# A wait for TensorE's own third-last matmul, and two more semaphore instructions, ahead of each run of 256-column matmuls

## What is computed

```python
def attn(x, w_in, conv_w, conv_b, w_B, w_C, w_out):
    xp, z = split(x @ w_in, 2)                    # 256 -> 2 x 512
    xc = silu(causal_conv(xp, conv_w) + conv_b)   # 4 taps per channel
    h_t = 0.9 * h_{t-1} + 0.1 * (xc_t @ w_B)      # 16 states
    return ((h @ w_C) * silu(z)) @ w_out          # 512 -> 256

def ffn(x, Wr, br, W1, b1, W2, b2):
    idx = top_k(x[:, 0, :] @ Wr + br, 2)          # by the first token of a batch entry
    h = gelu(x @ W1[idx] + b1[idx])               # two experts, 256 -> 256 each
    return sum(h @ W2[idx] + b2[idx]) / 2

x = x + attn(layernorm(x), ...)
x = x + ffn(layernorm(x), ...)
```

## Time and profile before

| what | us |
|---|---|
| median of 3 runs | 509.01 (508.89 to 509.17) |
| the profiled execution, its own time | 509.31 |
| its span, first to last instruction | 507.5 |
| TensorE busy | 503.0 (99%) |
| VectorE busy | 452.3 (89%) |
| ScalarE busy | 400.7 (79%) |
| GpSimd busy | 348.2 (69%) |

### The profile page before, as it was taken

One profiled execution on the slowest core, in us unless ns is written; L12 is line 12 of the kernel. 1 busy time (PEld: TensorE's weight loads), 2 busy tenths in 40 slices (PEclk: granted clock), 3 DMA queues, 4 the chain that ended last, 5 costly groups with the idle time before them and its releaser, 6 DMA issues.

```text
span 507.5 us, 9839 instructions
## 1 busy us (share of the span) xinstructions
PE 503.0 (99%) x3026; PEld 447.6 (88%) x3026; DVE 452.3 (89%) x896; ACT 400.7 (79%) x692; POOL 348.2 (69%) x390
## 2 busy tenths in 40 slices
PE   8999999999999999999999999999999999999997
PEld 8889799898898989989899998989989899998997
DVE  6999899999998899989999899998999989996773
ACT  4986958878869788697887969779797887969454
POOL 4959597659693796928969197772977649673391
PEclk9999999999999999999999999999999999999999
DMA  8940005344251432606235170432604333130102
GB/s 266 292 174 12 32 0 173 119 131 162 74 182 37 165 124 83 206 17 193 79 124 165 42 223 24 165 124 86 203 40 143 106 125 125 51 115 0 43 3 83
DMA packets 53379, 57.28 MB, mean 113 GB/s; under 512 B 8682, under 2 KB 49642, under 8 KB 53226
## 3 DMA queue, kind: packets, MB, share of 16 engines
q1 hardware_dynamic: 51498, 56.67, 34.1%
q10 hardware_dynamic: 1856, 0.31, 0.3%
HBM read 35.46 MB, written 21.50 MB: 112 GB/s over the span
## 4 chain that ended last, share of the span: by engine, by line
PE 97%; DVE 1%; DMA 1%; issue 0%; DVEq 0%
PE blk L1291 16%; PE blk L1292 16%; PE blk L1296 16%; PE tok L1410 12%; PE tok L1408 12%; PE tok L1409 12%; PE turn L1449 3%; PE turn L1452 3%; PE blk L1471 3%; PE turn L1239 1%; PE tok L1291 1%; PE tok L1296 1%; PE tok L1292 1%; DMA x_mid<-in_L_attn_x 1%; DVE stats_t L914 0%; DVE normed L931 0%
## 5 line engine op out<-in xcount | busy, mean ns | idle before, releaser
L989 DVE SCALAR_TENSOR_TENSOR conv<-blk,tap_w,conv 128x512 f32<-128x512 f32 x192 | 130.1, 740 | 8.2 <-ACT conv L680 7.6
L485 POOL TENSOR_TENSOR y_lo<-gate,y_hi 128x512 fp32r<-128x512 f32 x57 | 72.2, 1299 | 36.6 <-ACT y_hi L608 36.5
L1291 PE MATMUL blk<-xn_hi,w_in_hi 128*128 128x512 f32 x228 | 89.5, 393 | 0.0
L1292 PE MATMUL blk<-xn_hi,w_in_lo 128*128 128x512 f32 x228 | 89.1, 391 | 0.0
L450 POOL TENSOR_TENSOR xc_lo<-conv,xc_hi 128x512 fp32r<-128x512 f32 x60 | 72.7, 1229 | 8.3 <-ACT xc_hi L608 8.1
L1408 PE MATMUL tok<-w_out_hi,y_hi 128*128 128x256 f32 x256 | 72.1, 282 | 0.0
L1410 PE MATMUL tok<-w_out_hi,y_lo 128*128 128x256 f32 x256 | 71.9, 281 | 0.0
L1409 PE MATMUL tok<-w_out_lo,y_hi 128*128 128x256 f32 x256 | 71.9, 281 | 0.0
L1296 PE MATMUL blk<-xn_lo,w_in_hi 128*128 128x512 f32 x228 | 70.3, 389 | 0.0
L1408 PE MATMUL tok<-w_hi,hid_hi 128*128 128x256 f32 x248 | 69.9, 282 | 0.0
L1410 PE MATMUL tok<-w_hi,hid_lo 128*128 128x256 f32 x248 | 69.7, 281 | 0.0
(11 more groups left out here) (189 smaller groups left out, 1321.7 us busy)
## 6 DMA issues: line engine op xcount, KB each, us to landing
spill<-normed SPq DMA_DIRECT2D x25, 512.0 KB, 2.8
normed<-spill SPq DMA_DIRECT2D x100, 128.0 KB, 2.8
out<-x_mid SPq DMA_DIRECT2D x30, 256.0 KB, 2.7
x_mid<-in_L_attn_x SPq DMA_DIRECT2D x29, 256.0 KB, 2.7
x_in<-in_L_attn_x SPq DMA_DIRECT2D x14, 512.0 KB, 4.3
w_all<-in_L_ffn_W SPq DMA_DIRECT2D x2, 2048.0 KB, 11.8
b_all<-in_L_ffn_b SPq DMA_DIRECT2D x1, 1024.0 KB, 13.1
gate<-in_L_attn_w_in SPq DMA_DIRECT2D x2, 256.0 KB, 4.5
```

Source lines behind the costliest of these rows:

```text
L485: nc.gpsimd.tensor_tensor(y_lo[:, j, :], gate_of(o, j), y_hi[:, j, :].bitcast(F32), ALU.subtract).then_inc(y_lo_set, 1)
L989: nc.vector.scalar_tensor_tensor(cols, blk[j][:], tap_w[:, j, t:t + 1], cols, ALU.mult, ALU.add).then_inc(tap_added, 1)
L1291: mm(dst, whi(k), his(k), start=(k == 0), stop=False)
L1292: mm(dst, wlo(k), his(k), start=False, stop=False)
```

## The change

TensorE gets three semaphores that only its own matmuls raise: `x_tail` after the fourth of the six matmuls of the last `xp` block, `state_tail` after the second of the four L1452 matmuls of `state_in`, and `up_tail` after the fourth matmul of the last `up` block in steps 16 and 17. Each time two 512-column matmuls are still to come behind the raised one, so it is the third-last of its run. A new function `behind()` stands after the old waits and ahead of the first 256-column matmul. It raises a counter `paced` that nobody waits for, waits for the tail semaphore, and raises `paced` three times more. In the built program that is four semaphore instructions: the first carries the old waits (done, y_lo_set or g_lo), the second carries the new wait, the third and the fourth carry nothing. In the loop the count to wait for is worked out in a register, for `x_tail` just ahead of the second. Nothing else is changed, and no matmul moves.

```diff
+PACE = 3
...
+        x_tail, state_tail, up_tail = sem("x_tail"), sem("state_tail"), sem("up_tail")
+        paced = sem("paced")
...
-            def project(bank, whi, wlo, his, los, ready, c, sem_out):
+            def project(bank, whi, wlo, his, los, ready, c, sem_out, third_last=None):
...
-                    mm(dst, wlo(k), his(k), start=False, stop=False)
+                    ins = mm(dst, wlo(k), his(k), start=False, stop=False)
+                if third_last is not None:
+                    ins.then_inc(third_last, 1)
...
-                        (t1_hi, t1_lo) if part == 0 and j == 0 else None, a, sem_out)
+                        (t1_hi, t1_lo) if part == 0 and j == 0 else None, a, sem_out,
+                        x_tail if part == 0 and j == JD - 1 else None)
...
-                            (t2_hi, t2_lo) if j == 0 else None, f, up_ready)
+                            (t2_hi, t2_lo) if j == 0 else None, f, up_ready,
+                            up_tail if j == JF - 1 and not has_attn(s) else None)
...
+            def behind(tail, count):
+                pe.sem_inc(paced, 1)
+                pe.wait_ge(tail, count)
+                for _ in range(PACE):
+                    pe.sem_inc(paced, 1)
...
-            def down(f, h, js=range(JF)):
+            def down(f, h, js=range(JF), tail=None):
...
+                    if j == 0 and tail is not None:
+                        behind(*tail)
...
-            def out_proj(o, h):
+            def out_proj(o, h, tail=None):
...
+                    if j == 0 and tail is not None:
+                        behind(*tail)
...
                     ins = mm(bank[:], b_mix[:, j, :], xc_lo[:, j, :], start=False, stop=(j == JD - 1))
+                    if j == JD - 3:
+                        ins.then_inc(state_tail, 1)
...
-                out_proj(0, 0)
+                out_proj(0, 0, (x_tail, 3))
...
-                out_proj(1, 0)
+                out_proj(1, 0, (state_tail, 3))
...
-                    out_proj(o, 0)
+                    out_proj(o, 0, (x_tail, a + 1) if has_attn(s) else None)
...
-                    down(f, 0, (0, 1, 2))
+                    down(f, 0, (0, 1, 2), (up_tail, 2))
...
-                    down(f, 0, (0, 1, 2))
+                    down(f, 0, (0, 1, 2), (up_tail, 1))
...
-                down(f, 0)
+                down(f, 0, range(JF), (state_tail, a + 1))
```

## The result

The changed kernel takes **514.29 us** (median of 4 runs, 514.0 to 515.4) where the kernel before took 509.04 beside it (508.89 to 509.17): a ratio of 1.0108, 95% interval 1.0097 to 1.0120. It is 5.3 us slower. The forecast was 507.6 with a range that ended at 513.0, so direction and range were both missed. The profiled execution took 514.0 us, its span is 512.1, 4.6 more than before. The lines of the change have moved: L1292 is now L1295, L1296 is L1301, L1408 to L1410 are L1415 to L1417.

What follows compares the result with a forecast made beforehand. TensorE, busy 503.0 of 507.5 us, bounds the kernel. Gains net of lateness, 0.9 + 0.18 + 0 + 0.3 + 0.07 = 1.4 us, gave 507.9 profiled, 507.6 as median; range 504.5 to 513.0.

Steps and rivals of the forecast that it cites:

- the lateness of a place: At each of 30 places, first 256-column matmul starts 0.80 after the third-last's start, not 0.68: 0.12 lost, 3.6 us.
- The reaction: From the third-last matmul's end to the wait's release: 0.05 at the high end, left out of the 0.12.
- The bound of 0.17: High end of the loss at each of the 30 places: 0.05 added to 0.12 for the wait's release.
- The quick pace: Late loads put all places' 256-column streams at 0.1133 instead of 0.1178, saving 0.0044 per matmul: 507.6, chance 0.50.
- The rows that spoke against it: Two late starts that did not switch: after score matmuls (0.1175) and after transposes at 474.25 (0.118).
- The second: Rival: at each of the 30 first loads 0.12 is lost and the pace stays slow: 512.6, chance 0.22.
- The rule of the queue: TensorE's queue pulls weight loads ahead of matmuls in flight; the wait takes this lead away 30 times, giving nothing back.
- Half of the places switch: Rival: output projections turn quick, `down`s do not; 0.9 + 0.18 gained, 1.8 lost: 509.8, called 510, chance 0.15.
- The change does nothing: Rival: the load comes at 0.65, still hidden; nothing is lost and nothing switches: 509.0, chance 0.13.

Runs made afterwards that it cites:

- one extra instruction: Changed kernel with one more semaphore instruction at the start of TensorE's work, shifting later instructions in memory: 514.40 us, ratio 1.0106.
- the kernel with one increment: Changed kernel with PACE 1 instead of 3, leaving only the instruction that waits: 509.04 us, ratio 1.0001 against the kernel before.
- the output projections alone: Changed kernel with the wait taken out of `down`, so only the 15 output projections wait: 509.84 us, ratio 1.0018 against the kernel before.

## Why the prediction was wrong

**The bound was right.** TensorE sets the end, and what its program adds between two matmuls is paid in full. The table's last two columns bear it out.

**The step that failed is the lateness of a place:** 0.39 + 0.30 + 0.11 = 0.80 against 0.68, hence 0.12, times 30 = 3.6 us. Measured 0.234, times 30 = 7.0: 3.4 us too little. Its parts: the matmul's record, 0.39, and the step from load to matmul, 0.11, were right. The reaction, for which I took nothing, is 0.04 (0.431 less 0.39). The three instructions, priced at 0.1 each by the earlier trace rows, take 0.15 + 0.15 + 0.076 = 0.376 from the first one's start to the load; had they only waited, it would have been 0.111 + 0.111 + 0.076 = 0.298, the 0.30 that I took. So the 0.12 that was missing per place is 0.04 of reaction and 0.08 of increments. The earlier trace rows shows two instructions that only wait; those of the change also increment. I took the nearest row and did not see that it lacked the one thing that these do. The Trainium skill, "Perfetto Trace Analysis", section "Sequencer-only Instruction (DRAIN, etc)", says that the push of a semaphore update comes after the reported end and before the next instruction is fetched. The traces agree: the record is 0.051 either way, the next start 0.150 behind one that increments and 0.111 behind one that doesn't. The bound of 0.17 had no row with an increment behind it, and the 0.064 beyond it, thirty times, are 1.9 us, more than the 1.3 by which the range was missed.

**The quick pace as such was right.** Its sizes were met: 5.35 for 47 distances of an output projection (expected 5.35), 3.99 for the stretch of `down` less its first distance (3.98), the stretch of 48 unchanged at 10.91, the 12 behind `state_out` slow. I had it everywhere, for 5.0 us; the changed kernel got 3.1, since the ten output projections of the loop stayed slow. That is 1.9 us more. The rows that spoke against it were the better guide. The opening adds 0.9 in the profiled execution. From the forecast for a profiled execution, 507.9, that is 507.9 + 3.4 + 1.9 + 0.9 = 514.1, for the 514.0 that it took.

**The rivals.** The second, late and slow, ended on the right side for a wrong reason: 512.6 was 0.12 per place and no quick pace at all. With the measured lateness it would have given 516, which only the profiled execution with one extra instruction came near (515.7). The rule of the queue that stood beside it, in the Trainium skill, "TensorE: Matmul & The Clock Gate", section "Step-by-step: what each phase is for", gets the loss and not the return. "Half of the places switch" named the output projections as those that would; it was the `down`s that all switched, and ten of the 15 output projections that didn't. "The change does nothing" is the kernel with one increment, to the hundredth (509.04).

**What stays open** is what chooses the pace. Not the size of the lateness (4 ns were enough in one kernel, 385 ns failed at 26 places in another), not the load's instant alone (within a trace one instant always went with one pace, but 0.808 was quick in the changed kernel and slow with one extra instruction ahead), not the loop as such, since the same ten places were quick in it with the output projections alone. Moving the instructions in memory re-dealt the paces in the traced executions, and left the medians of the changed kernel where they were; whether it is the place in memory, or each execution's own start, or the chip, these runs can't say, since only one execution of each kernel was traced. Why the changed kernel's other three runs took 514.2 and more, if the opening's wait was the profiled one's alone, is open too.

## What to carry to other kernels

Where a wait on the critical engine repeats N times, price it from a row with the same kind of instruction, and carry N times the doubt into the range: here one incrementing instruction more or less moved the result from 0.4% faster to 1.1% slower. A wait that lets the next weight load start just ahead of its matmul costs nothing and can still change the pace of the stream behind it. A gain that hangs on which of two paces a stream settles in should be measured with the program shifted as well, as it may be luck.

## What the hardware showed that I had not expected

- A stream of 256-column matmuls runs at 0.1178 or at 0.1133 us each and keeps its pace until it ends or a load in it comes late, and 1 to 2 ns in the first steps go with one or the other (loads at 0.580 to 0.581 slow, 0.582 to 0.583 quick in one trace). No stream was quicker than 0.113. The Trainium skill, "TensorE: Matmul & The Clock Gate", section "Back-to-back issue gap", has a formula for a single matmul's gap by which an estimate for 256 columns is 109.2 ns. No trace here shows that; the measured pace decides.
- On TensorE's sequencer the next instruction starts 0.150 us behind a semaphore instruction that increments and 0.111 behind one that only waits, though both have a record of 0.051; a weight load starts 0.076 behind either.
- A semaphore instruction with two waits, of which the first was met long before, begins its record early and waits inside it (1988 ns at one place). When the second wait is met it ends at once, 0.437 after the third-last matmul's start, and the load comes at 0.570, 0.048 earlier than the distances above give for an instruction that starts at 0.431.
